# One batch of masked attention on three engines, its work in another order

## The reference

```python
x = x + _L0_gnn_ref(_layernorm(x), adj, Wq, bq, Wk, bk, Wv, bv, Wo, bo)
x = x + _L0_ffn_ref(_layernorm(x), controller, f1, f2)

# _L0_gnn_ref, for each batch and each of 8 heads of 32 features:
scores = einsum('bhqd,bhkd->bhqk', q, k) / sqrt(32)
scores = where(adj == 0, -inf, scores)        # the same adj (256 x 256) for all batches
out = einsum('bhqk,bhkd->bhqd', softmax(scores), v)
return out @ Wo.T + bo
```

## Time and profile before

| | before |
|---|---|
| median of 3 runs | 793.73 us |
| lowest, highest | 792.57, 794.19 us |
| the profiled execution, its time | 795.41 us |
| its span (first to last instruction) | 793.2 us |
| TensorE matmul busy | 737.7 us, 93% |
| VectorE busy | 608.9 us, 77% |
| ScalarE busy | 564.6 us, 71% |
| GpSimd busy | 125.4 us, 16% |
| granted TensorE clock, mean | 0.985 |

### The profile page before, as it was taken

The page is one execution under the profiler, slowest core; times in us unless marked ns, Lnnn a source line. Parts: engine busy times, 40 slices in busy tenths (PEclk is TensorE's granted clock), DMA queues, the critical chain, the costliest instruction groups (busy, mean ns, idle before and its releaser), DMA issues.

```text
span 793.2 us, 22744 instructions
## 1 busy us (share of the span) xinstructions
PE 737.7 (93%) x7408; PEld 572.9 (72%) x7408; DVE 608.9 (77%) x2558; ACT 564.6 (71%) x1654; POOL 125.4 (16%) x125
## 2 busy tenths in 40 slices
PE   7699999999999999999999999988989989987948
PEld 6588888888888888888888888755555555653636
DVE  5589899899999999998999998877656647645612
ACT  3689998999899899899989998855454444542500
POOL 1101001000100100010010001636325225100000
PEclk9999999999999999999999999999999999999969
DMA  5775676576566656765765665730589989989989
GB/s 159 164 182 135 142 176 148 126 176 152 139 160 150 165 135 150 177 146 128 177 145 132 151 149 130 221 99 2 236 307 320 388 289 304 388 293 302 379 302 322
DMA packets 102262, 157.61 MB, mean 199 GB/s; under 512 B 12352, under 2 KB 65088, under 8 KB 101952
## 3 DMA queue, kind: packets, MB, share of 16 engines
q1 hardware_dynamic: 99744, 155.04, 68.4%
q10 hardware_dynamic: 2464, 1.84, 1.0%
HBM read 47.78 MB, written 41.94 MB: 113 GB/s over the span
## 4 chain that ended last, share of the span: by engine, by line
PE 81%; DMA 10%; DVE 3%; SPq 2%; ACT 2%; issue 1%; DVEq 0%; ACTq 0%
PE bank L524 14%; PE bank L476 14%; PE bank L538 8%; PE bank L511 7%; PE bank L561 7%; PE bank L498 7%; PE bank L709 6%; DMA stage<-scratch 6%; PE bank L688 5%; PE bank L677 3%; SPq L317 2%; PE bank L735 2%; DMA scratch<-stage 2%; PE bank L781 2%; PE bank L552 2%; PE bank L469 2%
## 5 line engine op out<-in xcount | busy, mean ns | idle before, releaser
L853 ACT ACTIVATE Ps<-Ps,nmax 128x256 f32<-128x256 f32 x512 | 255.7, 505 | 2.7 <-DVE nmax L1052 2.7
L1052 DVE CUSTOM_DVE_ANT_0 Ps<-bank,masks 128x256 f32<-128x256 f32 x512 | 196.0, 420 | 8.7 <-issue 7.0
L524 PE MATMUL bank<-ident,Ps 128*128 128x128 f32 x1024 | 142.1, 277 | 2.7 <-ACT Ps L853 2.2
L524 PEld LDWEIGHTS bank<-ident,Ps 128*128 128x128 f32 x1024 | 113.2, 141 | 34.6 <-issue 24.7
L476 PE MATMUL bank<-hT,WT 128*128 128x256 f32 x512 | 116.1, 379 | 2.3 <-ACT hT L810 2.3
L511 PE MATMUL bank<-stack 128*128 128x256 f32 x512 | 107.3, 321 | 5.1 <-DMA stack<-parts 5.1
L397 POOL TENSOR_TENSOR X<-X,bob 128x512 f32 (+1 forms) x32 | 40.7, 1273 | 421.4 <-ACT hn L818 402.0
L476 PEld LDWEIGHTS bank<-hT,WT 128*128 128x128 f32 x512 | 94.8, 190 | 14.5 <-ACT Vs L826 1.8
L1063 DVE COPY PTs<-bank 128x512 f32<-128x512 f32 x128 | 87.8, 686 | 18.3 <-PE bank L524 18.3
L409 POOL TENSOR_SCALAR h<-X,mv,roots 128x256 f32<-128x256 f32 x64 | 80.2, 1265 | 118.1 <-PE bank L677 82.7
L853 ACT ACTIVATION_READ_ACCUMULATOR Ps<-Ps,nmax 128x1 f32 x512 | 98.8, 193 | 0.0
(11 more groups left out here) (88 smaller groups left out, 1071.1 us busy)
## 6 DMA issues: line engine op xcount, KB each, us to landing
stack<-parts SPq DMA_DIRECT2D x508, 128.0 KB, 2.4
scratch<-stage SPq DMA_DIRECT2D x64, 512.0 KB, 4.1
stage<-scratch SPq DMA_DIRECT2D x48, 512.0 KB, 5.7
X<-in_x SPq DMA_DIRECT2D x32, 256.0 KB, 2.8
out<-X SPq DMA_DIRECT2D x32, 256.0 KB, 5.0
XRlast<-scratch SPq DMA_DIRECT2D x8, 1024.0 KB, 12.1
f1s<-in_L_ffn_f SPq DMA_DIRECT2D x1, 2048.0 KB, 9.1
f2s<-in_L_ffn_f SPq DMA_DIRECT2D x1, 2048.0 KB, 14.1
```

The lines of the kernel that those rows point to most:

```text
L524: last = nc.tensor.transpose(PTb[h % 2][:, k * N + t * P:k * N + t * P + P], Ps[:, pr % 2, t, h % 2, k * P:k * P + P], ident[:, :])
L853: last = nc.scalar.activation(Ps[:, pr % 2, t, h, :], Ps[:, pr % 2, t, h, :], ACT.Exp, bias=nmax[:, pr % 2, t, h:h + 1], scale=-1.0, accum ...
L1052: last = nc.vector.tensor_tensor_reduce(out=Ps[:, pr % 2, t, h, :], in0=s_bank(n)[:, h * N:h * N + N], in1=masks[:, t, :], scale=1.0, scal ...
```

## The change

The calls in `batch` of three engines stand in another order; nothing is computed otherwise, and no instruction of the loop is added or removed. The order of one batch in the middle, with the steps that move:

- TensorE before: s0, K, Q, s1, p6 and p7 of the batch before, s2, s3, V, s4, s5, r, p0, p1, pv 1 of the batch before, p2, p3, s6, s7, O, p4, hT, pv 0, p5.
- TensorE after: s0, s1, p6, p7, Q, K, s2, pv 1 of the batch before, s3, s4, r, p0, p1, V, s5, s6, p2, p3, s7, O, p4, hT, p5, pv 0.
- ScalarE before: norm, K, Q, e0, pt7 of the batch before, e1, e2, rbc, e3, pt1, e4, V, e5, pt3, e6, hT, e7, pt5.
- ScalarE after: norm, pt7, Q, e0, K, e1, rbc, e2, e3, pt1, V, e4, pt3, e5, e6, e7, pt5, hT.
- VectorE before: statistics (every second batch), m0, low K, m1, m2, low Q, pt6 of the batch before, m3, pt0, m4, normalise, m5, m6, pt2, m7, residual, pt4, statistics of the result, reciprocals.
- VectorE after: m0, pt6, statistics (every second batch), m1, low Q, low K, m2, m3, pt0, normalise, m4, m5, pt2, m6, m7, residual, pt4, statistics of the result, reciprocals.

The small norm steps move with their neighbours. `save_high` waits for the stacking DMAs of two batches before in the save that now comes first (Q).

```diff
@@ TensorE, batch @@
-                if not (first or last):
-                    k_project(b + 1)
-                if not last:
-                    q_project(b + 1)
                 scores(b, par, 1)
                 if not first:
                     p_transpose(prev(b), 6)
                     p_transpose(prev(b), 7)
+                if not last:
+                    q_project(b + 1)
+                if not (first or last):
+                    k_project(b + 1)
                 scores(b, par, 2)
+                if not first:
+                    pv(prev(b), 1 - par, 1)
                 scores(b, par, 3)
                 if last:
                     pe.wait_ge(ctl_in, 16)
                     logits(0, M[0])
-                if not last:
-                    v_project(b + 1)
                 scores(b, par, 4)
-                scores(b, par, 5)
                 if not first:
                     r_transpose(prev(b), last)
                 p_transpose(b, 0)
                 p_transpose(b, 1)
-                if not first:
-                    pv(prev(b), 1 - par, 1)
+                if not last:
+                    v_project(b + 1)
+                scores(b, par, 5)
+                scores(b, par, 6)
+                if last:
+                    one_hot_transpose(0, M[0])
                 p_transpose(b, 2)
                 p_transpose(b, 3)
-                if last:
-                    one_hot_transpose(0, M[0])
-                scores(b, par, 6)
                 scores(b, par, 7)
...
+                p_transpose(b, 5)
                 pv(b, par, 0)
-                p_transpose(b, 5)
@@ ScalarE @@
-                if which == 1 or isinstance(b, int) and b == 0:
+                if which == 0 or isinstance(b, int) and b == 0:
...
+                if not first:
+                    save_pt(prev(b), 7)
                 if last:
                     save_h2T(0, (M[0], M[1]))
                 if not last:
-                    save_k(b + 1, 1 - par)
                     save_q(b + 1, 1 - par)
                 exps(b, 0)
-                if not first:
-                    save_pt(prev(b), 7)
+                if not last:
+                    save_k(b + 1, 1 - par)
                 exps(b, 1)
-                exps(b, 2)
                 if not first:
                     save_rbc(prev(b))
+                exps(b, 2)
                 exps(b, 3)
                 save_pt(b, 1)
-                exps(b, 4)
                 if not last:
                     save_v(b + 1, 1 - par)
-                exps(b, 5)
+                exps(b, 4)
                 save_pt(b, 3)
                 if last:
                     save_one_hot(0, M[0])
+                exps(b, 5)
                 exps(b, 6)
+                exps(b, 7)
+                if last:
+                    save_h2T(1, (M[0], M[1]))
+                save_pt(b, 5)
                 if not late:
                     save_hT(b + 2)
-                if last:
-                    save_h2T(1, (M[0], M[1]))
-                exps(b, 7)
-                save_pt(b, 5)
@@ VectorE @@
+                maximum(b, 0)
+                if not first:
+                    save_pt(prev(b), 6)
                 if ahead:
                     sums_of(b + 3)
                     mean_variance(mv, 2 * QT)
-                maximum(b, 0)
+                maximum(b, 1)
                 if not last:
-                    save_low(b + 1, 1 - par, 1, 0)
-                    save_low(b + 1, 1 - par, 1, 1)
-                maximum(b, 1)
+                    for which in range(2):
+                        for g in range(G):
+                            save_low(b + 1, 1 - par, which, g)
                 maximum(b, 2)
...
+                if not first:
+                    normalise(prev(b))
                 maximum(b, 4)
```

More of the change, by code:

```diff
@@ L1179, in batch @@
                     mean_variance(mv, 2 * QT)
-                maximum(b, 0)
+                maximum(b, 1)
                 if not last:
-                    save_low(b + 1, 1 - par, 1, 0)
-                    save_low(b + 1, 1 - par, 1, 1)
-                maximum(b, 1)
+                    for which in range(2):
+                        for g in range(G):
+                            save_low(b + 1, 1 - par, which, g)
                 maximum(b, 2)
-                if not last:
-                    save_low(b + 1, 1 - par, 0, 0)
-                    save_low(b + 1, 1 - par, 0, 1)
-                if not first:
-                    save_pt(prev(b), 6)
                 maximum(b, 3)
@@ L1199, in batch @@
                     one_hot(0)
-                if not first:
-                    normalise(prev(b))
-                maximum(b, 5)
                 norm_step(0)
-                maximum(b, 6, lambda: norm_step(1))
+                maximum(b, 5, lambda: norm_step(1))
                 norm_step(2)
@@ L1207, in batch @@
                 norm_step(3)
-                maximum(b, 7, lambda: norm_step(4))
+                maximum(b, 6, lambda: norm_step(4))
                 norm_step(5)
+                maximum(b, 7, lambda: norm_step(6))
                 if not first:
                     residual(prev(b))
-                norm_step(6)
+                norm_step(7)
                 save_pt(b, 4)
-                norm_step(7)
+                norm_step(8)
                 if not first:
-                    sums_of_result(prev(b), lambda: norm_step(8))
+                    sums_of_result(prev(b), lambda: norm_step(9))
                     mean_variance(mvr, QT)
-                    norm_step(9)
+                norm_step(10)
+                if not first:
                     keep_statistics(prev(b))
-                norm_step(10)
                 reciprocals(b, lambda: norm_step(11))
```

## The result

The changed kernel takes 809.7 us (median of four runs, 808.17 to 810.42), the kernel before 793.96 us in the runs beside it. The ratio is 1.0207, with a 95% interval of 1.0182 to 1.0232. The forecast was 807.6 us in a range of 797 to 815.

A forecast was written before the change was run, and what follows sets the result against it. TensorE was taken to bound the kernel. Per batch 0.31 + 0.05 + 0.10 = 0.46 us, 13.3 over batches 1 to 29, plus 0.6 at the ends: +13.9 us, giving 807.6 us, range 797 to 815.

The forecast's parts named there:

- e2: ScalarE's exponentials number 2 of a batch, now behind rbc: claimed to find m2 about 0.4 us early.
- e5: ScalarE's exponentials number 5 of a batch, needed by p4: claimed to let p4 start 6.07 us behind r's end.
- The bound and the mechanism: Loop: TensorE bounds without gaps; the new order makes p4 wait for e5 every batch; +13.9 us in all.
- Rival A: Loop: ScalarE's stretch is 0.31 us shorter than read, TensorE stays the bound, only exits are paid; 797.2 us, chance 0.09.
- B: Loop: TensorE stays the bound, pv's exits into scores cost no more than into transposes; 794.3 to 785.6 us, chance 0.08.
- rival C: Loop: VectorE's low K and m2 late beyond a 0.4 us cover, delaying e2 and p4; 816.3 us at 0.3 beyond, chance 0.09.
- The wait: Each loop batch, ahead of p4: ScalarE's list gives 6.07 us behind r, TensorE is ready after 5.76, so 0.31 us.
- The weights behind the wait: At p4 in each loop batch: transposes starting behind a wait can't hide their weights, 0.05 us more.
- The exits: Both pv groups, now followed by scores: 0.20 us each instead of 0.15 into transposes, 0.10 us more a batch.
- Batch 0: First batch: p4 already waited for e5, and pt3 now stands ahead of e5 as one more copy; +0.5 us.
- the clock: Falling TensorE clock: no rival with a share of its own, since the wait is 0.3 us in a round of 16.
- The end: Batches 30 and 31: batch 30's 0.46 us is swallowed, batch 31 bounded by -1 to +1.5; taken as +0.1 us.

The follow-up runs named there:

- the second measurement: The changed kernel measured once more, unaltered, beside others on the same chip: 809.33 us, ratio 1.0224.
- the two kernels without a wait: Changed kernel with e5 ahead of pt3: 796.99 us; that plus both pv groups followed by transposes and hT's copy ahead of pt5: 796.76 us.
- the two pair kernels: New order on three engines, both pv groups side by side, against the kernel before: 789.37 us; with batch 31's own lists and batch 30's low K moved: 788.32 us.
- the last kernel: Order with both pv groups side by side, plus batch 31's own lists and batch 30's low K ahead of m2: 788.32 us, 0.9929 against the kernel before.
- the pair's first kernel: New order on three engines with both pv groups side by side, no special last batch: 789.37 us, 0.9971 against the kernel before.
- the overlong filler: Changed kernel plus 8 unread matmuls ahead of s2 and 12 behind s4, batch 0 alone: 810.78 us, ratio 1.0255.
- the short one: Changed kernel plus 5 unread matmuls ahead of s2 and 5 behind s4, batch 0 alone: 810.24 us, ratio 1.0204.

## Why the prediction was right, and where it wasn't

**The bound and the mechanism: right.** The forecast sum was +13.9 us, the profiled executions differ by 15.0, the medians by 15.7 (on the chip of the second measurement by 17.6). In the loop it was 13.3 against 13.8 measured, and the place, the engine, the count and the cause were those named: p4 waits for e5, in every batch, because ScalarE's list from rbc on is longer than TensorE's stretch from r to p4. Rival A (ScalarE just fits) and B (pv's exits are free) fell with the wait itself; rival C (VectorE late at m2) fell in the loop: among ScalarE's waits between 60 and 500 us there is none of an exponential for VectorE. It was nearer than the prediction had it, 0.27 us instead of 0.4.

**The wait: 0.31 said, 0.39 found.** The length of ScalarE's list was read right; what was too small is the last link. The prediction took 0.06 us from the end of the accumulator's reading to p4, from batch 0. In the hardware loop it is 0.12:

```profile
217.46 0.21 ACT L853 ACTIVATION_READ_ACCUMULATOR Ps<-Ps,nmax 128x1 f32 x1
```

This ends at 217.67 and p4 starts at 217.80; the chain above calls it "issue", 0.12 us, and it is 0.12 to 0.13 in all batches from 2 to 27. In batches 0, 1 and 28 to 31, which are written out ahead of and behind the hardware loop, it is 0.05 to 0.06. So this link makes 26 x 0.06 = 1.6 us.

**The weights behind the wait: right.** 0.05 said, 0.04 found; from p4's start to hT's it is 0.48, as against 224.62 to 225.06, 0.44, before.

**The exits: 0.10 said, 0.06 found.** The step of 0.05 each was sized from the weight loads of scores and transposes; the two kernels without a wait that differ in what follows pv (15.56 and 15.50) give 0.06 for both; they also differ in the place of hT's copy, but that ends 0.57 us ahead of Q's weights already in the first, so it can't be what the 0.06 is. The chain's rows say 0.67 - 0.48 = 0.19 for an exit into scores, against 0.15 into transposes, so 0.04 each. By the Trainium skill, page "TensorE: Matmul & The Clock Gate", section "LDWEIGHTS (loading the stationary operand)", loading goes by the number of columns alone. With equal loads the two exits would cost the same; here they don't, though the difference is no larger than that of the loads, 0.05. The Trainium skill's page "TensorEngine Tiling (Array Packing)", section "Key Properties", says that a change of tiling mode drains TensorE; the trace agrees in that leaving the tile shape costs time, 0.15 or 0.19 us for each exit, and the batch is 0.2 to 0.3 us shorter in the order in which two stays in pv become one (15.50 to 15.22 and 15.30).

**Batch 0: 0.5 said, 3.7 found. This is the step that failed.** Two things were missed in it. The prediction looked only at p4's own predecessor, pt3, and didn't walk the chain of batch 0 anew: in it there is no r, and no pv ahead of p0, V was what filled TensorE's time ahead of p0, and K's save had been free. That gives the estimated 1.2 instead of 0.5. And it dismissed the clock, because the loop's wait is 0.3 us in 16; it was right for the loop, where the granted clock is 1.00, but batch 0 has holes of 2.34, 1.43 and 1.20 us one behind the other. In all seven profiles of this batch 0 without filler (in some of them with one more call moved) the clock was at 0.50 for a part of the time between 32 and 39 us; in the four profiles with the old batch 0 (the kernel before among them, the two pair kernels without its pv) it was at 1.00 there. An earlier fall, from 27.1 to 27.7 until 30.5 to 31.1, came in three profiles of both orders and cost less: batch 0 took 13.53 us in the last kernel, which has it, and 12.92 in the pair's first kernel, which has the same batch 0 without it. So the order and the later fall go together; which trait of the order brings it (the holes, or V's place behind them) wasn't separated; that filling the holes prevents it is shown only by the overlong filler, which cost as much as it gave back, and by the short one, behind an earlier fall.

**The end: +0.1 said, -0.8 found in the first profile, +0.8 in the second,** both within the bounds of -1 and +1.5; the two differ in whether the clock falls from 530 to 540 us. Which of batch 31's moves gains wasn't tried. Behind attention the difference of -1.3 us is not the change's: that part lasts 260.6 to 263.8 us in the profiles of all these kernels, though its instructions are the same.

So of the 1.5 us by which the sum was short against the profiled execution's 15.4 in the span, batch 0 was 3.2 too low and the wait 2.1 (26 x 0.08), the exits 1.0 too high (29 times 0.10 less 0.065), the last two distances 0.9 and the part behind attention 1.3 too high; 0.6 too high is that the 29 distances of the kernel before have a mean of 15.52 us and not the 15.495 of the middle of the loop. The total is better than its parts: misses of both signs cancelled, which is luck and not method. In the second profile they cancelled otherwise (2.0 ahead of the first O, 13.6, 0.8 and -2.3) to 14.2.

## What to carry to other kernels

Where two engines are near the bound, an order is judged by its closed loops: start at the point where the bounding engine releases the other (here r), add up both lists until they meet again (here p4), and compare; the difference is paid in every round, and a single exchange on the slower list gives it back. Look at the next loop too (here K, its low half, m2, e2): it may lie only 0.24 us behind. Moving rbc shortened the first loop alone and brought nothing; moving pt3 shortened the end of the list, which both loops share, and brought 0.44 us. Walk the same chain once more for the first and the last batch, because what hides a step in the loop isn't there, and a hole there can bring the clock down. Gains in TensorE's own time, like one stay in a small tile shape instead of two, count only when the other engines' lists still fit.

## What the runs showed of the hardware that was not expected

- From the end of an accumulator's reading on ScalarE to the start of the waiting matmul it is 0.12 to 0.13 us in every batch of the hardware loop and 0.05 to 0.06 in the batches written out ahead of and behind it. What makes the difference wasn't tried.
- Three holes of 2.34, 1.43 and 1.20 us within 9 us came with a granted clock of 0.50 for 6.8 us, and three holes in each of six more profiles of this batch 0 with 0.50 for 3.4 to 6.8 us; in three profiles (one of these seven, one with a filler, one with the old batch 0) it fell already at 27.1 to 27.7, just behind the first hole, and was up again by 31.1.
- A 128 x 128 matmul of two fp32 operands took 0.24 us, a transpose of the same size 0.11.
- Pv's 32 matmuls in one piece take 1.86 us, in two 2.00 and a second exit of 0.15 to 0.19.
